# A megakernel of modulated convolutions and routed experts: GpSimd's order of scaling and listing, and the place of the hrow transposes

## The reference: what is computed

```python
def _layer(x, style, w, b, mw, mb, typ):
    s = style @ mw.T + mb
    weight = SCALE * w * s[:, None, :, None]
    demod = lax.rsqrt(jnp.sum(weight * weight, axis=(2, 3)) + EPS)
    weight = weight * demod[:, :, None, None]
    ...
scores = jax.nn.sigmoid(x @ gate_w.T) + bias
topk_w, topk_idx = jax.lax.top_k(scores, TOPK)
topk_w = topk_w / (jnp.sum(topk_w, axis=-1, keepdims=True) + 1e-20)
...
out = jnp.einsum('eti,ehi->th', zw, Wd)
out = out + jax.nn.silu(x @ Sg.T) * (x @ Su.T) @ Sd.T
...
x = x + ffn(cond(x, cond_512, ...), ...)
```

## Time and profile before

| | us |
|---|---|
| median of 3 runs | 1262.66 |
| lowest and highest | 1261.30, 1268.32 |
| the profiled execution | 1263.14 |
| its span, first to last instruction | 1261.3 |
| busy: TensorE matmuls | 1146.1 (91%) |
| busy: TensorE weight loads | 1008.8 (80%) |
| busy: VectorE | 805.2 (64%) |
| busy: GpSimd | 576.1 (46%) |
| busy: ScalarE | 495.3 (39%) |

### The profile page before, as it was taken

How to read it: one execution, slowest core, us unless ns; L and a number is a source line. 1 busy time by engine, 2 the same in 40 slices (tenths; PEclk the granted TensorE clock), 3 DMA queues, 4 the chain that set the end, 5 groups by cost and what they waited for, 6 DMA issues and landing times. The chain is left out here.

```text
span 1261.3 us, 24476 instructions
## 1 busy us (share of the span) xinstructions
PE 1146.1 (91%) x7149; PEld 1008.8 (80%) x7150; DVE 805.2 (64%) x1947; ACT 495.3 (39%) x1149; POOL 576.1 (46%) x667
## 2 busy tenths in 40 slices
PE   4899898999989898863999999999999999999995
PEld 2787676777767677642999999999998899999995
DVE  8777676767767675754665565655657565555653
ACT  4656455545555454421332232323233332222321
POOL 2100423233241405164565656666665565666663
PEclk9999999998989998965999999999999999999998
DMA  6755555554545454314667667666766777666664
GB/s 225 175 152 149 120 133 134 133 133 116 143 102 145 112 136 106 85 43 115 149 120 154 120 150 120 133 138 115 159 112 154 190 126 157 110 108 114 111 113 75
DMA packets 140376, 163.58 MB, mean 130 GB/s; under 512 B 31456, under 2 KB 97088, under 8 KB 138816
## 3 DMA queue, kind: packets, MB, share of 16 engines
q0 software_dynamic: 35696, 74.34, 33.0%
q1 hardware_dynamic: 104320, 88.63, 26.0%
q10 hardware_dynamic: 336, 0.32, 0.1%
HBM read 74.58 MB, written 55.18 MB: 103 GB/s over the span
## 5 line engine op out<-in xcount | busy, mean ns | idle before, releaser
L1262 PE MATMUL bank<-xt_hi,wup_hi 128*128 128x256 f32 x1104 | 278.3, 285 | 1.9 <-issue 1.9
L1262 PE MATMUL bank<-xt_hi,wup_lo 128*128 128x256 f32 x1104 | 278.0, 284 | 0.0
L461 POOL DMA_INDIRECT out_rows<-yb,sid x140 | 225.5, 1611 | 90.0 <-DVE yb L1045 66.0
L409 POOL DMA_INDIRECT lists<-entry,place x128 | 128.8, 1006 | 196.4 <-DVE place L859 153.6
L1262 PEld LDWEIGHTS bank<-xt_hi,wup_hi 128*128 128x128 f32 x1104 | 212.6, 193 | 6.2 <-issue 3.7
L1262 PEld LDWEIGHTS bank<-xt_hi,wup_lo 128*128 128x128 f32 x1104 | 213.2, 193 | 2.4
L544 ACT ACTIVATE t<-bank,cB,cA 128x256 f32<-128x256 f32 (+1 forms) x384 | 172.0, 534 | 98.8 <-PE bank L221 96.3
L448 POOL DMA_INDIRECT xg<-h_rows,gid x140 | 141.8, 1013 | 120.7 <-PE bank L1240 77.1
L1266 PE MATMUL bank<-xt_lo,wup_hi 128*128 128x256 f32 x1104 | 178.1, 284 | 0.0
L1045 DVE TENSOR_SCALAR yb<-bank,all_lists 128x512 f32<-128x512 f32 x138 | 99.9, 748 | 87.0 <-DMA out_rows<-yb,sid 55.0
L1266 PEld LDWEIGHTS bank<-xt_lo,wup_hi 128*128 128x128 f32 x1104 | 152.7, 193 | 0.0
(11 more groups left out here) (204 smaller groups left out, 2164.5 us busy)
## 6 DMA issues: line engine op xcount, KB each, us to landing
x<-x1p SPq DMA_DIRECT2D x64, 384.0 KB
wraw<-in_Wup SPq DMA_DIRECT2D x11, 1024.0 KB, 7.7
xraw<-in_xq SPq DMA_DIRECT2D x32, 260.0 KB, 2.8
xbase<-in_x SPq DMA_DIRECT2D x32, 256.0 KB, 2.8
h_rows<-hrow SPq DMA_DIRECT2D x128, 64.0 KB, 2.2
out_rows<-orow SPq DMA_DIRECT2D x32, 256.0 KB, 2.1
x<-x1p SPq DMA_DIRECT2D x64, 127.0 KB
wdraw<-in_Wdn SPq DMA_DIRECT2D x11, 512.0 KB, 9.8
```

The lines of the kernel that those rows point to most:

```text
L409: pool.indirect_dma_start(out=lists, out_offset=bass.IndirectOffsetOnAxis(ap=place[:, home, r, k:k + 1], axis=0), in_=entry[:, home, r, k, ...
L461: pool.indirect_dma_start(out=out, out_offset=bass.IndirectOffsetOnAxis(ap=sid[:, u:u + 1], axis=0), in_=yb[:, u, :], in_offset=None, comp ...
L1262: pe.matmul(dst, lhs[a], rhs[0], start=k == 0 and a == 0, stop=False)
```

## The change

GpSimd: ten inputs instead of eight are scaled ahead of the rounds and the rest two groups further ahead. In each quarter of a turn the scaling stands first, and the round's entries follow in shares of one, two, one and no groups. The waits for x2 and x3 between the scatters are gone; `place_ready` is waited for in the first quarter, behind that quarter's scaling. The last full round has a place and entry slot of its own (3), and its `mark` waits for no scatters. TensorE turns hrow behind layer 0 and in front of layer 1; ScalarE and VectorE make xt_hi and xt_lo between the two phases of layer 2's inputs (t2 and x2).

```diff
--- before.py
+++ after.py
@@ -161,8 +161,8 @@
         key_i = sb("key_i", [P, R, TOPK], I32)
         lane_i = sb("lane_i", [P, R, TOPK], I32)
         col_i = sb("col_i", [P, R, TOPK], I32)
-        place = sb("place", [P, 3, R, TOPK], I32)
-        entry = sb("entry", [P, 3, R, TOPK, 2])
+        place = sb("place", [P, 4, R, TOPK], I32)
+        entry = sb("entry", [P, 4, R, TOPK, 2])
 
         cnt = sb("cnt", [P, E])
         over = sb("over", [P, E, E])
@@ -410,28 +410,30 @@
                         out=lists, out_offset=bass.IndirectOffsetOnAxis(ap=place[:, home, r, k:k + 1], axis=0),
                         in_=entry[:, home, r, k, :], in_offset=None).then_inc(S[done], 16)
 
-            for g in range(2, 2 * R):
+            for g in range(2, 2 * R + 2):
                 scaled(g, g % 2, g // 2)
 
-            with pool.Fori(0, ROUNDS - 1) as it:
-                coming = lambda r: (it * R + (2 * R + r), r % 2, it * (R // 2) + (2 * R + r) // 2)
+            shares = ((0,), (1, 2), (3,), ())
+            with pool.Fori(0, ROUNDS - 2) as it:
                 for r in range(R):
+                    scaled(it * R + (2 * R + 2 + r), r % 2, it * (R // 2) + (R + 1 + r // 2))
                     if r == 0:
-                        scaled(*coming(0))
-                        scaled(*coming(1))
                         pool.wait_ge(S["place_ready"], it + 1)
-                    else:
-                        pool.wait_ge(S["x2_ready" if r == 2 else "x3_ready"], it * (4 * R) + 4 * (R + 3 + r // 2) + 4)
-                    scatter(2, r, "scattered")
-                    if r == 1 or r == 2:
-                        scaled(*coming(r + 1))
-            assert (ROUNDS - 1) * R + 2 * R == G
+                    for n in shares[r]:
+                        scatter(2, n, "scattered")
+            assert (ROUNDS - 2) * R + 2 * R + 2 == G - 2
+            for r in range(R):
+                if r < 2:
+                    scaled(G - 2 + r, r % 2, G // 2 - 1)
+                if r == 0:
+                    pool.wait_ge(S["place_ready"], ROUNDS - 1)
+                for n in shares[r]:
+                    scatter(2, n, "scattered")
             pool.wait_ge(S["place_ready"], ROUNDS)
-            scatter(2, 0, "scattered")
+            scatter(3, 0, "scattered")
             for r in range(R):
                 if r:
-                    pool.wait_ge(*((S["x3_ready"], (LAST + 1 + r) * 4 + 4) if LAST + 1 + r < G else (S["h_ready"], G)))
-                    scatter(2, r, "scattered")
+                    scatter(3, r, "scattered")
                 pool.wait_ge(S["place_ready"], ROUNDS + r + 1)
                 scatter(r % 2, 0, f"scattered{r % 2}")
 
@@ -565,18 +567,18 @@
 
                 if within(g, 0, G - 1):
                     layer0(g + 1)
-                if conv:
-                    for ph in range(2):
+                for ph in range(2):
+                    if ph == 1 and stage:
+                        act.wait_ge(S["xt_t"], g - 1)
+                        act.activation(xt[0][:, 0].rearrange("p q (b c) -> p q b c", b=NB),
+                                       bank[5][:].rearrange("p (b q c) -> p q b c", b=NB, q=Q), ACT.Copy).then_inc(S["xt_hi"], 1)
+                    if conv:
                         act.wait_ge(S["l1_done"], g * 2 + (ph + 1))
                         if not (first and g == 0):
                             act.wait_ge(S["x2_ready"], g * 4 - 2 + 2 * ph)
                         land(act)
                         evac(g, (2 * ph, 2 * ph + 1), bank[1 + ph][:].rearrange("p (b w) -> p b w", b=2),
                              t2[:, 2 * ph:2 * ph + 2, :], 1, S["t2_ready"])
-                if stage:
-                    act.wait_ge(S["xt_t"], g - 1)
-                    act.activation(xt[0][:, 0].rearrange("p q (b c) -> p q b c", b=NB),
-                                   bank[5][:].rearrange("p (b q c) -> p q b c", b=NB, q=Q), ACT.Copy).then_inc(S["xt_hi"], 1)
                 if within(g, 1, G + 1):
                     act.wait_ge(S["l3_done"], g)
                     if not (first and g < 3):
@@ -874,14 +876,14 @@
 
                 def routing():
                     if many:
-                        places(number, 2 if many == R else (number - ROUNDS - 1) % 2, many)
+                        places(number, (number - ROUNDS - 1) % 2 if many < R else 3 if early else 2, many)
                     if stage and early and g > LAST:
                         last = g - LAST - 1
                         choose(ROUNDS + last, 1 if last else R)
                         if last:
                             mark((last - 1) % 2, (f"scattered{(last - 1) % 2}", 16 * TOPK) if last > 2 else None, 1)
                         else:
-                            mark(2, ("scattered", 16 * TOPK * R * (ROUNDS - 1) + 16), R)
+                            mark(3, None, R)
                     elif not early and u == 0:
                         choose(it + 1, R)
                     elif not early and u == 1:
@@ -889,8 +891,13 @@
 
                 if within(g, 0, G - 1):
                     layer0(g + 1)
-                if conv:
-                    for ph in range(2):
+                for ph in range(2):
+                    if ph == 1 and stage:
+                        dve.wait_ge(S["xt_hi"], g - 1)
+                        turned = lambda a: a[:, 0].rearrange("p q (b c) -> p q b c", b=NB)
+                        dve.tensor_tensor(turned(xt[1]), bank[5][:].rearrange("p (b q c) -> p q b c", b=NB, q=Q),
+                                          turned(xt[0]).bitcast(F32), ALU.subtract).then_inc(S["xt_lo"], 1)
+                    if conv:
                         dve.wait_ge(S["t2_ready"], g * 2 + (ph + 1))
                         two = slice(2 * ph, 2 * ph + 2)
                         ends = t2[:, two, 0:W:W - 1]
@@ -899,11 +906,6 @@
                         dve.tensor_copy(x2[0][:, two, :, 0:V], blocks).then_inc(S["x2_ready"], 1)
                         dve.wait_ge(S["x2_ready"], g * 4 + (2 * ph + 1))
                         minus(x2[1][:, two, :, 0:V], blocks, x2[0][:, two, :, 0:V]).then_inc(S["x2_ready"], 1)
-                if stage:
-                    dve.wait_ge(S["xt_hi"], g - 1)
-                    turned = lambda a: a[:, 0].rearrange("p q (b c) -> p q b c", b=NB)
-                    dve.tensor_tensor(turned(xt[1]), bank[5][:].rearrange("p (b q c) -> p q b c", b=NB, q=Q),
-                                      turned(xt[0]).bitcast(F32), ALU.subtract).then_inc(S["xt_lo"], 1)
                 if stage:
 
                     dve.wait_ge(S["sg_ready"], g - 1)
@@ -1115,6 +1117,14 @@
                 odd = g % 2 if early else (R + 1 + u) % 2
                 if within(g, 0, G - 1):
                     layer0(g + 1)
+                if stage:
+
+                    pe.wait_ge(S["h_ready"], g - 1)
+                    if not (early and g == 2):
+                        pe.wait_ge(S["o_ready"], g - 2)
+                    for c in range(HC):
+                        r = pe.transpose(bank[5][:, P * c:P * c + P], hrow[:, odd, c, :], ident[:])
+                    r.then_inc(S["xt_t"], 1)
                 if conv:
 
                     if early and g == 0:
@@ -1131,14 +1141,6 @@
                         pe.wait_ge(S["x1_stacked"], (g + 1) * (16 * STACKS))
                         hi_passes(pe, dst, terms)
                         lo_passes(pe, dst, terms).then_inc(S["l1_done"], 1)
-                if stage:
-
-                    pe.wait_ge(S["h_ready"], g - 1)
-                    if not (early and g == 2):
-                        pe.wait_ge(S["o_ready"], g - 2)
-                    for c in range(HC):
-                        r = pe.transpose(bank[5][:, P * c:P * c + P], hrow[:, odd, c, :], ident[:])
-                    r.then_inc(S["xt_t"], 1)
                 if within(g, 1, G + 1):
 
                     if not (early and g == 1):
```

## The result

The changed kernel takes 1230.40 us in the median (1229.53 to 1231.99, 4 runs), the one before 1262.57: a ratio of 0.9738, interval 0.9707 to 0.9769, 32 us less. The forecast was 1242.6 with a range of 1224 to 1256. The way and the mechanism hold; the gain is 1.6 times what was forecast.

A forecast was written before the change was run, and what follows sets the result against it. TensorE's first-half groups, stalled once a round behind GpSimd's list entries, set the time; the new bound is a 15.5 us cycle. -18.7 over 27 groups and -1.3 behind them make -20.0: 1242.6 us, range 1224 to 1256.

The forecast's parts named there:

- Scaling first takes the stall away: First half: GpSimd scaling before list entries removes a 5.5 us stall in each of six rounds, 33 us.
- The waits for xt go, a wait for orow comes: TensorE: xt waits near nothing; transposes wait for orow 0.3 to 1.3 us in nearly every group, 20 to 30 in sum.
- A group is 10.57 + D: Cycle of one 128-row group: hand-over 0.15, TensorE's 9.02 and layer 1's 1.40, plus D; forecast 15.5 us.
- D: Time from turning z to the end of VectorE's orow: 4.27 plus 0.65 of delay by GpSimd's scaling, 4.92 us.
- the group "without waits": An early group of the kernel before, from which 9.02 us from transposes to turning z was taken as TensorE's own.
- The tail: The two groups after 490.89: xt_lo comes sooner, the orow wait is paid; -1.3 us, between 0 and -3.7.
- the hand-over: From the end of VectorE's orow to TensorE's start: 0.15 us in each group.
- TensorE alone bounds at 14.33: Rival: TensorE's own work alone sets a group at 14.33 us; kernel 1211; chance 0.03.
- the missed port: Rival: scalings miss VectorE's x3 work in every group, D 4.27, a group 14.84; kernel 1225; chance 0.16.
- The clock: Rival: each TensorE wait of about 1.1 us is followed by 1.2 GHz; kernel 1278; chance 0.05.
- The late input: Rival: place_ready a group late in turn 0, so ScalarE stands as now; kernel 1276; chance 0.04.
- Early groups: First-half groups that had no stall: lengthened from 14.3 to about 15.4 us, about 1.2 lost each.

The follow-up runs named there:

- E8: The new GpSimd order alone, transposes behind layer 1 and both xt evacuations as in the kernel before: 1230.97 us, ratio 0.9752 to the kernel before.
- E9: The change with the hrow transposes put back behind layer 1, xt evacuations still split: 1198.84 us, ratio 0.9489 to the kernel before.
- E10: The change with one added wait holding GpSimd's scaling until x3 is written: 1209.99 us, ratio 0.9581 to the kernel before.
- E11: The kernel before with early turning of hrow and split xt evacuations alone, GpSimd as it was: 1264.56 us, ratio 1.001.
- E3: The change with transposes back behind layer 1, evacuations split, on the chip where the kernel before took 1272.08: 1238.84 us, ratio 0.9735.
- E4: The change with scaling held until x3 is written, on the chip where the kernel before took 1272.08: 1250.08 us, ratio 0.9819.

## Why the prediction was right, and where its sizes were off

- **Scaling first takes the stall away: right.** E8 has no zt_hi wait over 0.5 us, GpSimd idles before each input, and the clock stays up. The forecast for this part was 33 us: E8 is at 32 (35 in its 27 groups).
- **The waits for xt go, a wait for orow comes: right.** 34.1 us in 31 groups, 0.9 to 1.2 each in the 27 and 1.8 in two behind them; 0.3 to 1.3 each were forecast. The forecast sum of 20 to 30 was too low by its own terms: 4.92 + 0.15 - 3.91 is 1.16 a group, 36 us in 31 groups.
- **A group is 10.57 + D: right in form, off in one term.** The step that failed is "the rest is TensorE's: 9.02 from the transposes to turning z in a group without waits". It measured 8.51 in E9. With layer 1's 1.40 the term is 9.9 to 10.0 (9.99 in the group above), not 10.42. Over 27 groups the 0.44 are 11.9 us, against a miss of 12.2. What the group "without waits" held was a wait for xt_hi (E9 above).
- **D: right cause, size a little low.** I took 4.92, it was 5.03 in the mean: 3.0 us the other way. The guess that the scaling would move up to 1 us forward against x3 was wrong in most groups: it starts 1.3 to 2.7 us after turning z (351.05 less 348.60 is 2.45 in the group above) and mostly catches a whole step. E10 settles that this is a cost: 20 us for removing it, and D falls to the forecast's lower bound of 4.27. The forecast counted this delay only in front of the transposes; E8 shows that with the transposes in their old place it reaches TensorE too, by way of xt (0.6 us where groups can be compared).
- Together: -18.7 - 11.9 + 3.0 is -27.6, measured -29.2. Of the other 1.6 us, 0.4 is the stretch before, which is 439.40 by this mark and not 439.04, and 0.7 the hand-over, 0.12 in the mean and not 0.15. **The tail** was forecast -1.3 and is -2.1.
- **TensorE alone bounds at 14.33: wrong for the same reason.** It is 13.82.
- **Rivals.** The time lies near the missed port's 1225, but not by its mechanism: the port was hit in every one of the 27 groups (D 4.86 to 5.16). The clock stayed at 1.00 beside waits of about 1.1 us, 27 times in a row. The late input did not come, GpSimd had 2.2 us or more to spare.
- Early groups were forecast at 15.4 and took 14.9 to 15.2, against 14.3 to 14.7 before. Against E8 the second part of the change costs 1.6 us over the first four of the 27 groups and 4.2 over the others, and saves only in the two behind them. E8 and E11 show it to be worth nothing as it stands, and E9 that half of it, the split evacuations, is worth 32 us when the other half is left out.

The Trainium skill (SBUF — State Buffer, SBUF: two separate sides) says that the port pair shared by VectorE and GpSimd is an exclusive lock, held for a whole instruction while the other engine blocks. The trace agrees with its 0.94 us of a 64x4 subtraction beside a scaling of 1.05, and its 0.17 in E10.

## What to carry to other kernels

Before an operation is issued earlier, ask what holds its output buffer: the transposes came 1.4 us sooner and ran into the bank that an older group's result had not left, and the work between had been the cover for that. Make the inputs of a late consumer earlier on the side engines, and leave the producer where its buffer is free. For a "clean" duration of TensorE, compare the distances between starts with those of the same matmuls elsewhere; a row that prints no idle time can hide a third of a microsecond in each group.

## What the runs showed that was not expected

- The wait that idle times hide: 0.5 us in a group between the transposes and turning z, and with it a floor of 13.82 instead of 14.33 us a group.
- A VectorE delay that layer 1 hides from the transposes comes back in E8 as waits for xt_hi and xt_lo in the next group, 0.6 us at the one place of the loop where groups with and without it can be compared.
- How small a VectorE step can be and still pay for a whole GpSimd instruction: 64x4, 0.17 to 0.94 us.
- One chip of four on which ScalarE stood 5 to 7 us once per round in front of sg, in the orders of E3 and E4. The kernel before was 0.75% slower on it (1272 against 1262 to 1263) and the new orders up to 3.3% (1250 against 1210). What ScalarE waited for there stays open.
